# Picking the last pairs' expert results on TensorE instead of gathering them, with the shared experts split around the rounds

## The chip, the cores and the metric

The kernel runs on one core of a Trainium2 chip. The metric is the device time of one execution in microseconds (us); lower is better. Every time below comes from the hardware profiler or from timed runs on the chip.

## What is computed

One tower with three stages, all in float32. Stage one is a masked tokenizer, stage two a small attention layer, stage three a mixture of experts with top-2 routing and two shared experts:

```python
W = weight * mask[None]                       # (16, 5000, 128)
h = einsum('bg,egp->bep', x, W) + bias        # 64 batches x 16 tokens x 128
h = h + attention(layernorm(h))               # 8 heads, causal over 16 tokens
xf = layernorm(h).reshape(-1, 128)            # 1024 tokens
scores = sigmoid(xf @ gate_w.T)               # 64 experts, top 2 each
y[e] = (silu(buf[e] @ w1[e]) * (buf[e] @ w3[e])) @ w2[e]
routed = sum over the 2 experts of y * score * 2.5 / sum of the 2 scores
shared = (silu(xf @ sw1) * (xf @ sw3)) @ sw2
out = h + shared + routed
```

## The kernel before, in words

It is written in direct per-engine programs: each of the five engines (TensorE `pe`, VectorE `dve`, ScalarE `act`, GpSimd `pool`, SyncE `sp`) has its own list of instructions, which it runs strictly in the order in which they are written. The engines wait for each other by semaphores alone. A late instruction therefore holds all that stands behind it on its engine.

The 1024 tokens are eight **pairs** (chunks of 128 tokens, `NCH = 8`). In the tail of the program j, k and l are pairs 5, 6 and 7. The tokenizer streams 65 MB of weights through a ring buffer, masks them on VectorE and GpSimd and sums them on TensorE (L843) until about 157 us. The attention and the routing of earlier pairs run beside it. What is left then is the attention of pairs 6 and 7, the routing of pairs 5 to 7, and the experts.

**Routing.** For each pair VectorE picks the top two experts (`choose`), TensorE counts ranks (`rank_tokens`), VectorE computes for each token two slot numbers (`place`), and GpSimd scatters the token rows by indirect DMA to these slots in device memory (`scatter`, L486). SyncE loads the slots back (`load_slots`, L399).

**The experts run in two rounds** of groups of 512 slots. Round one (groups 0 to 7) has pairs 0 to 4 with 64 slots per expert, round two (groups 8 to 11) has pairs 5 to 7 with 32 slots per expert. Each group goes through: `turn_xs` (transpose on TensorE, L989 or in round two L993), `copy_xsT` (ScalarE, L696), `up` (L1015), `silu` (ScalarE, L704 and L705), `mid` (gate product: GpSimd L508 in round one, VectorE L1411 in round two), `turn_mid` (L1029), `copy_midT` (L711), `down` (L1045), `copy_y` (L715), `store_group` (SyncE to device memory, L405). Pair 7 is not scattered: VectorE marks its slots as one-hot rows (`mark_slots`, L1361 and L1362) and TensorE adds its tokens into round two's transposed inputs (`add_last`, L999).

**Collecting.** GpSimd gathers each token's two result rows from device memory by indirect DMA (`gather`, L533, two per pair, 16 in all), round one's pairs when round one's stores have landed, pairs 5 to 7 when round two's stores have landed. VectorE multiplies by the weights and adds (`combine`, L1429 and L1430, two instructions per pair), SyncE writes out two pairs at a time with two DMAs (L430). The weights come from `score_exp` (ScalarE, L725) and `weights` (VectorE, L1417 to L1422).

**The shared experts** (`shared_up` L1056, `silu_shared` L721, `shared_mid` L1400, `shared_down` L1064, `add_shared` L1405) run in two halves of four pairs, both after the last `down`. Their weights sw1, sw3 and sw2 arrive by three DMAs of SyncE (L415 to L417), which stand behind four `load_slots`, a piece of w2 (L389) and a 1 MB table of slot numbers (L414).

**The stretch around the change on TensorE** is `turn_xn(l)`, `turn_xs(0)`, `project(l)` (L865), `spin(3)`, `turn_xs(1)`, `spin(3)`, `turn_xs(2)`, `up(0)`, `up(1)`, `turn_xs(3)`, `turn_qk(l)`. `spin(n)` (L928) issues n matmuls whose result nobody reads. ScalarE has there `copy_xnT(l)` (L610), `copy_xsT(0)`, `copy_xsT(1)`, `square_qk(l)` (L599), `norm_qk(l)` (L605, L606), `probs(k)` (L641). `probs(k)` is the exponential that VectorE's `weigh_values(k)` (L1292, L1293) waits for. The norms' inverse square roots are powers on GpSimd (`root_*`, L455). In the trace a plain float32 matmul shows as two instructions (four calls of L993 are x8), a transpose as one (four calls of L989 are x4).

Of the kernel before, what the change touches and what calls it, by code (L numbers as in the profile page):

```python
# [19 lines left out]
ALU = mybir.AluOpType  # L20
# [7 lines left out]
P = 128  # L28
# [20 lines left out]
GATHERED_EARLY = NCH1  # L49
# [42 lines left out]
def M_BANK(g):  # L92
    return 4 if g < GROUPS1 else (3, 4)[g % 2]
# [6 lines left out]
def S_BANK(i):  # L100

    return ((1, 5, 7), (0, 2, 3))[i]
# [69 lines left out]
def tower_kernel(nc, x, tok_w, tok_b, tok_mask, W_dq, W_uq, W_qr, W_dkv, W_ukv, W_kr, W_o,  # L172
                 q_ln_g, q_ln_b, kv_ln_g, kv_ln_b, gate_w, w1, w3, w2, sw1, sw3, sw2, consts, masks, out):
    with ExitStack() as ctx:
# [8 lines left out]

        bank = [ctx.enter_context(nc.psum_tensor(f"bank{i}", [P, 512], F32)) for i in range(8)]
# [45 lines left out]
        wts = sb("wts", [P, NCH, 2])  # L230
        msel = sb("msel", [P, NCH, E], BF16)
# [21 lines left out]
        ssil, shs = ring_view(18304, 512), ring_view(18816, 512)  # L253

        hm = [mask[:, 256 * i:256 * (i + 1)].rearrange("p (i h) -> p i h", h=H) for i in range(2)]
        gt = [mask[:, 512 + 256 * i:768 + 256 * i].rearrange("p (i h) -> p i h", h=H) for i in range(2)]
        slot_iota, hot = xT[:, 0:M_SLOTS], prod[:, 0:M_SLOTS]
# [62 lines left out]
        s_iota, s_hot = sem("slot_iota_in"), sem("last_slots_marked")  # L320

# [31 lines left out]
        def _(sp):  # L353
# [59 lines left out]
            load_w2(0, (0, WREM), (0, S))  # L413
            sp.dma_start(slot_iota, masks[:, M_W:M_W + M_SLOTS]).then_inc(s_iota, 16)  # L414
            sp.dma_start(sw13[:, 0, :], sw1).then_inc(s_sw, 16)  # L415
            sp.dma_start(sw13[:, 1, :], sw3).then_inc(s_sw, 16)
            sp.dma_start(sw2s, sw2).then_inc(s_sw, 16)  # L417
            for g in range(STORED_FIRST):
                store_group(g)
# [3 lines left out]
            for g in range(STORED_FIRST, GROUPS):  # L423
                store_group(g)
# [20 lines left out]
        def _(pool):  # L445
            pool.memset(half[:], -0.5).then_inc(s_pool, 1)
            pool.memset(zeros, 0.0).then_inc(s_zsrc, 1)
            pool.wait_ge(s_ones, 1)
# [67 lines left out]
            root_h2(j)  # L516
            mid(0)
            mid(1)
            mid(2)
# [6 lines left out]
            scatter(k)  # L526
            root_h2(l)
            mid(7)

# [8 lines left out]
            pool.wait_ge(s_slot, NCH - 1)  # L538
            pool.wait_ge(s_yout[0], 16 * GROUPS1)
            for j in range(GATHERED_EARLY):  # L540
                gather(j)
            pool.wait_ge(s_ys, GROUPS)
            for j in range(GATHERED_EARLY, NCH1):
                gather(j)
            pool.wait_ge(s_gidx, 1)
            pool.wait_ge(s_yout[1], 16 * (GROUPS - GROUPS1))
            for j in range(NCH1, NCH):
                gather(j)

        @block.scalar  # L550
        def _(act):
# [155 lines left out]
            def copy_midT(g):  # L707
# [3 lines left out]
                act.copy(hT[g % 2], bank[M_BANK(g)][:, 0:PG * H]).then_inc(s_hT, 1)  # L711
# [106 lines left out]
        def _(pe):  # L818
# [201 lines left out]
            def turn_mid(g):  # L1020
                pe.wait_ge(s_hm, g + 1)
                if g >= 1:
                    pe.wait_ge(s_hT, g if g <= GROUPS1 else g - 1)
# [531 lines left out]
```

## Time and profile before

| what | us |
|---|---|
| median of 3 timed runs (lowest, highest) | 241.35 (240.23, 242.11) |
| the profiled execution, its own time | 241.4 |
| its span, first to last instruction | 239.7 |
| TensorE busy / VectorE busy / GpSimd busy | 184.3 / 152.4 / 145.6 |
| last tokenizer matmul | about 157 |
| last `down` matmul of round two | about 220.3 |

The span leaves out 1.7 us that the profiled execution has around it (241.4 - 239.7). Times in rows count from the span's start. Rows of a timeline or of the chain of waits read: start, duration, engine, line.

### The profile page before, as it was taken

The page shows a single profiled execution, that of the slowest core. Times are in us where ns is not written, and L with a number is a line of the kernel's source. Part 1 is how long each engine was busy: PE and PEld are TensorE (multiplying, and loading weights), DVE is VectorE, ACT ScalarE, POOL GpSimd, SP SyncE. Part 2 cuts the span into 40 slices and gives each one's busy share as a digit, 9 for nine tenths or more (in the row PEclk, how much of TensorE's full clock was granted, in tenths as well). Part 3 has the DMA queues.
Part 4 walks back from the last instruction along what each step waited for, and adds up shares of the span by engine and source line. Part 5 has one row for each costly group of instructions (what it writes and reads, how often), then busy time and mean ns, then how long its engine had stood idle before and what let it go on. Part 6 is the DMA issues. An engine that isn't in the chain of part 4 may idle for free.

```text
span 239.7 us, 6216 instructions
## 1 busy us (share of the span) xinstructions
PE 184.3 (77%) x2549; PEld 154.8 (65%) x2549; DVE 152.4 (64%) x366; ACT 82.7 (35%) x245; POOL 145.6 (61%) x117
## 2 busy tenths in 40 slices
PE   0057969558989969979879789699997989999700
PEld 0056949457878958857758767588776767767400
DVE  0024384686497796897996994978999627410571
ACT  2005200003324324324133124136878744344400
POOL 3326469519998949879969949620161651375360
PEclk9999997977999989999999999999999999999975
DMA  6989999999999999999999999949901329234241
GB/s 220 290 311 417 362 419 384 346 421 415 421 413 417 420 418 420 414 427 418 403 408 228 234 218 191 153 87 303 263 0 44 115 68 296 68 98 121 71 112 35
DMA packets 32982, 65.12 MB, mean 272 GB/s; under 512 B 2874, under 2 KB 25367, under 8 KB 32375
## 3 DMA queue, kind: packets, MB, share of 16 engines
q1 hardware_dynamic: 31416, 59.47, 75.0%
q10 hardware_dynamic: 576, 3.26, 3.4%
q0 software_dynamic: 960, 1.97, 3.1%
q8 instruction: 21, 0.34, 0.6%
q14 instruction: 9, 0.07, 0.1%
HBM read 56.96 MB, written 7.73 MB: 270 GB/s over the span
## 4 chain that ended last, share of the span: by engine, by line
PE 32%; DVE 24%; DMA 18%; SPq 9%; ACT 6%; issue 5%; POOL 3%; POOLq 1%; DVEq 0%; ACTq 0%
DMA ring<-in_L_tok_weight_dram 16%; PE bank L843 10%; DVE ring L1241 5%; SPq L362 4%; DVE bank L1271 4%; PE bank L1045 3%; DVE prod L1262 3%; PE bank L1015 3%; DVE prod L1293 2%; DVE bank L1301 2%; SPq L368 2%; PE bank L993 2%; PE bank L999 2%; PE bank L928 2%; POOL rstd L455 2%
## 5 line engine op out<-in xcount | busy, mean ns | idle before, releaser
L466 POOL TENSOR_TENSOR ring<-ring,mask 128x896 f32<-128x896 f32 (+1 forms) x48 | 91.5, 1935 | 18.7 <-DMA ring<-in_L_tok_weight_dram 18.6
L843 PE MATMUL bank<-ring,xT 128*64 128x128 f32 x1248 | 84.3, 294 | 11.3 <-DVE ring L1241 8.0
L843 PEld LDWEIGHTS bank<-ring,xT 128*64 128x64 f32 x1248 | 76.4, 149 | 16.0 <-DVE ring L1241 12.8
L1241 DVE TENSOR_TENSOR ring<-ring,bank 128x1024 f32<-128x1024 f32 (+1 forms) x45 | 45.8, 1049 | 35.4 <-DMA ring<-in_L_tok_weight_dram 35.4
L455 POOL TENSOR_TENSOR rstd<-mv,half 128x1 f32<-128x1 f32 (+1 forms) x24 | 14.4, 603 | 32.4 <-DVE mv L1249 21.5
L533 POOL DMA_INDIRECT ring<-expert_outputs,slot_index x16 | 16.2, 1010 | 16.6 <-DMA expert_outputs<-ring 12.4
L824 PE MATMUL bank<-cst,w 64*128 64x64 f32 x39 | 5.3, 328 | 15.6 <-DMA w<-in_x_dram 14.8
L486 POOL DMA_INDIRECT expert_inputs<-xf,slot_index x14 | 14.3, 1022 | 4.3 <-issue 3.5
L508 POOL TENSOR_TENSOR mask<-ring,mask 128x256 f32<-128x256 f32 x8 | 7.5, 938 | 14.4 <-ACT ring L705 11.4
L824 PEld LDWEIGHTS bank<-cst,w 64*128 64x128 f32 x39 | 5.0, 219 | 15.7 <-issue 14.8
L579 ACT ACTIVATE offset<-shift,rstd 128x1 f32<-128x1 f32 x16 | 4.7, 292 | 25.1 <-POOL rstd L455 25.1
L1015 PE MATMUL bank<-w,ring 128*64 128x128 f32 (+1 forms) x256 | 12.9, 277 | 0.5 <-ACT ring L705 0.4
L1045 PE MATMUL bank<-w2p,ring 64*64 64x128 f32 (+1 forms) x256 | 12.8, 272 | 0.3 <-ACT ring L715 0.2
L1271 DVE TENSOR_REDUCE bank<-prod 128x16 f32<-128x288 f32 (+7 forms) x8 | 12.1, 1511 | 0.3
L1015 PEld LDWEIGHTS bank<-w,ring 128*64 128x64 f32 (+1 forms) x256 | 10.1, 123 | 2.6 <-ACT ring L696 1.1
L1045 PEld LDWEIGHTS bank<-w2p,ring 64*64 64x64 f32 (+1 forms) x256 | 10.2, 120 | 2.3 <-issue 1.2
L1293 DVE TENSOR_TENSOR prod<-vcat,bank 128x256 f32<-128x256 f32 (+7 forms) x8 | 10.8, 1344 | 0.0
L1301 DVE TENSOR_REDUCE bank<-prod 128x128 f32<-128x256 f32 (+7 forms) x8 | 10.6, 1321 | 0.0
L1262 DVE TENSOR_TENSOR prod<-kcat,bank 128x256 f32<-128x256 f32 (+5 forms) x6 | 6.5, 1089 | 4.8 <-ACT vcat L635 4.8
L1336 DVE MAX8 top<-bank 128x8 f32<-128x64 f32 x8 | 1.9, 232 | 12.0 <-PE bank L914 12.0
L715 ACT COPY ring<-bank 128x512 f32<-128x512 f32 x12 | 7.0, 585 | 7.0 <-PE bank L1045 7.0
L928 PE MATMUL bank<-cst 128*128 128x128 f32 x70 | 9.4, 279 | 0.0
(153 smaller groups left out, 297.4 us busy)
## 6 DMA issues: line engine op xcount, KB each, us to landing
ring<-in_L_tok_weight_dram SPq DMA_DIRECT2D x48, 832.0 KB, 13.5
expert_inputs<-w ACTq DMA_DIRECT2D x3, 1024.0 KB, 10.6
ring<-expert_inputs SPq DMA_DIRECT2D x6, 512.0 KB, 5.4
expert_outputs<-ring SPq DMA_DIRECT2D x12, 256.0 KB, 2.7
mask<-in_L_tok_mask_dram SPq DMA_DIRECT2D x3, 832.0 KB, 15.6
w<-in_x_dram SPq DMA_DIRECT2D x1, 1250.0 KB, 13.0
w2p<-in_L_ffn_w_dram SPq DMA_DIRECT2D x1, 1024.0 KB, 19.2
xT<-masks_dram SPq DMA_DIRECT2D x1, 1024.0 KB, 8.1
```

Of the source, the lines that this page charges most:

```text
L455: pool.tensor_tensor(rstd[:, a:b], mv[:, a:b, 1], half[:, 0:b - a], ALU.pow).then_inc(s_rstd, 1)
L466: pool.tensor_tensor(unit(j, q, SPLIT(q // 2), UC), unit(j, q, SPLIT(q // 2), UC), mask[:, (m + SPLIT(q // 2)) * D:(m + UC) * D], ALU.mult ...
L486: pool.indirect_dma_start(out=xs_dram[j // NCH1], out_offset=bass.IndirectOffsetOnAxis(ap=s_idx[:, j, k:k + 1], axis=0), in_=xf[:, j, :], ...
L533: pool.indirect_dma_start(out=yg[:, 2 * j + k, :], out_offset=None, in_=ys_dram[r], in_offset=bass.IndirectOffsetOnAxis(ap=s_idx[:, j, k:k ...
L843: last = pe.matmul(bank[0][64 * par:64 * par + 64, 0:D], xT[:, (UC * t + c) * B:(UC * t + c + 1) * B], unit(j, 2 * t + par, c, c + 1), sta ...
L928: pe.matmul(bank[where][:, 256:256 + P], ident, ident, start=True, stop=True)
L1015: last = pe.matmul(bank[U_BANK(g)][row:row + slots, tile * P:(tile + 1) * P], xsT[g % 2][:, n * slots:(n + 1) * slots], w13[:, EXPERT(g, n ...
L1045: last = pe.matmul(bank[Y_BANK(g)][row:row + slots, tile * D:(tile + 1) * D], hT[g % 2][H * par:H * par + H, tile * H + col:tile * H + col ...
L1241: dve.tensor_tensor(both(j, t, a, b), both(j, t, a, b), m.rearrange("p (u f) -> p u f", u=1).to_broadcast([P, 2, (b - a) * D]), ALU.mult). ...
L1271: then(dve.tensor_reduce(raw(j).rearrange("p (h s) -> p s h", h=NH), prod[:, 0:n * f].rearrange("p (s h d) -> p s h d", h=NH, d=DK), AX.X, ...
L1293: then(dve.tensor_tensor(prod[:, 0:n * D].rearrange("p (h d s) -> p h d s", d=DH, s=n), vcat[:, :, 0:n].rearrange("p (h d) s -> p h d s", ...
L1301: then(dve.tensor_reduce(o_raw(j), prod[:, 0:n * D].rearrange("p (f s) -> p f s", f=D), AX.X, ALU.add))
```

## The change

Pairs 6 and 7 are no longer gathered. For each of them there is a table of 2048 slots by 128 tokens in device memory, zeroed by SyncE (1 MB each). ScalarE makes two diagonal matrices of the pair's weights (`weight_rows`), GpSimd scatters their rows to the token's two slots (`scatter_picks`), SyncE loads the table back (`load_picks`), and TensorE multiplies it with round two's results as they stand on chip (`pick`, 8 matmuls of 128x128 per group). The sum stays in a bank, and VectorE adds it to the residual in one instruction. GpSimd's gathers are pairs 0 to 4 and then pair 5. The exponential for the late weights becomes a power on GpSimd (`late_exp`), `weights` is run for pairs 5 and 6 and then for pair 7, both earlier than before. The first half of the shared experts moves into round one: `shared_up(0)` before `turn_xs(0)`, its product to GpSimd, `shared_down(0)` behind `rank_tokens(k)`. Round two's transposes use `is_transpose=True`. The DMAs of sw1 and sw3 move ahead of the w2 piece, sw2 ahead of the slot table.

```diff
 # SyncE
+            sp.dma_start(sw13[:, 0, :], sw1).then_inc(s_sw, 16)
+            sp.dma_start(sw13[:, 1, :], sw3).then_inc(s_sw, 16)
             load_w2(0, (0, WREM), (0, S))
+            sp.dma_start(sw2s, sw2).then_inc(s_sw, 16)
             sp.dma_start(slot_iota, masks[:, M_W:M_W + M_SLOTS]).then_inc(s_iota, 16)
-            sp.dma_start(sw13[:, 0, :], sw1).then_inc(s_sw, 16)
-            sp.dma_start(sw13[:, 1, :], sw3).then_inc(s_sw, 16)
-            sp.dma_start(sw2s, sw2).then_inc(s_sw, 16)
+            sp.wait_ge(s_nopick, 1)
+            for table in pick_dram:
+                sp.dma_start(table..., no_picks...).then_inc(s_pickz, 16)
...
+            for g in range(STORED_FIRST, GROUPS1):
+                store_group(g)
+            load_picks(0)
+            sp.wait_ge(s_prod, NCH)
+            load_picks(1)
+            for g in range(GROUPS1, GROUPS):
                 store_group(g)
 # GpSimd
+            pool.memset(no_picks, 0.0).then_inc(s_nopick, 1)
             mid(0)
             mid(1)
+            pool.wait_ge(s_ssil, 1)
+            pool.wait_ge(s_shg, 1)
+            pool.tensor_tensor(shs, ssil, shg, ALU.mult).then_inc(s_shs, 1)
...
             scatter(k)
+            late_exp(NCH1, NCH - 1)
             root_h2(l)
             mid(7)
+            late_exp(NCH - 1, NCH)
+            for j in LATE:
+                scatter_picks(j)
...
-            for j in range(NCH1, NCH):
-                gather(j)
+            gather(NCH1)
 # ScalarE
             copy_xnT(l)
+            square_qk(l)
             copy_xsT(0)
             copy_xsT(1)
-            square_qk(l)
             norm_qk(l)
...
             copy_midT(8)
+            weight_rows(NCH - 1)
             copy_xsT(9)
 # TensorE
                 if i == 0:
                     pe.wait_ge(s_sw, 48)
-                    pe.wait_ge(s_hm, GROUPS)
+                    pe.wait_ge(s_xfTs, 4)
...
             turn_xn(l)
-            turn_xs(0)
+            spin(2, 7)
             project(l)
-            spin(3, 7)
+            shared_up(0)
+            turn_xs(0)
+            spin(3, 1)
             turn_xs(1)
...
             rank_tokens(k)
+            shared_down(0)
             turn_mid(4)
...
-            shared_up(0)
             shared_up(1)
-            shared_down(0)
+            pick(8)
+            pick(9)
+            pick(10)
             shared_down(1)
+            pick(11)
 # VectorE
             mark_slots(8)
+            dve.tensor_copy(s_idx[:, l, :], last_slot[:]).then_inc(s_gidx, 1)
+            weights(NCH - 1, NCH)
             mark_slots(9)
...
-            for j in range(4, NCH):
-                combine(j)
+            combine(4)
+            combine(5)
+            dve.wait_ge(s_picked, 1)
+            dve.tensor_tensor(fin[:, LATE[0]:, :], hres[:, LATE[0]:, :],
+                              bank[PICKED]..., ALU.add).then_inc(s_fin, len(LATE))
```

On TensorE, at the start of round one, these rows stand between the transpose of pair 7's normed tokens (L861, L927 after) and the transpose of group 1's slots. Before:

```order
L861 MATMUL bank3<-cst,qkn 128x128 [waits qkv_copied,xn]
L989 MATMUL bank2<-cst,ring 128x128 [waits xs_in0]
L989 MATMUL bank2<-cst,ring 128x128 x3
L865 MATMUL bank3<-wproj,xnT 128x149 [waits xnT_copied]
L928 MATMUL bank7<-cst 128x128 x3
L989 MATMUL bank2<-cst,ring 128x128 [waits xsT_copied]
```

And after (L1130 is `shared_up`, L1055 `turn_xs`, L994 `spin`):

```order
L927 MATMUL bank3<-cst,qkn 128x128 [waits qkv_copied,xn]
L994 MATMUL bank7<-cst 128x128 x2
L931 MATMUL bank3<-wproj,xnT 128x149 [waits xnT_copied]
L1130 MATMUL bank4<-xfT,ring 128x512 [waits xfT_copied,shared_w_in]
L1130 MATMUL bank7<-xfT,ring 128x512
L1055 MATMUL bank2<-cst,ring 128x128 [waits xs_in0]
```

The first shared matmul, with its wait for the shared weights, now stands ahead of every transpose of round one.

On SyncE the same DMAs stand in another order after the four slot loads. After the change:

```order
L415 DMA ring<-expert_inputs_1 128x8x128 x3
L429 DMA ring<-in_L0_ffn_sw1_dram 128x128 [waits third_summed]
L430 DMA ring<-in_L0_ffn_sw3_dram 128x128
L405 DMA w2p<-in_L0_ffn_w2_dram 16x16x128
L432 DMA ring<-in_L0_ffn_sw2_dram 128x128
L433 DMA xT<-masks_dram 128x2048
```

The three shared weights are behind the slot loads as before, sw2 also behind the w2 piece, and all three ahead of the 1 MB table.

On VectorE, in the routing of pair 7, the pieces behind the first pair of one-hot marks are after the change:

```order
L1454 TENSOR_SCALAR prod<-xT,last_slot 128x512 [waits slots,slot_iota_in]
L1455 SCALAR_TENSOR_TENSOR prod<-xT,last_slot,prod 128x512 [waits vector_chain]
L1563 CAST slot_index<-last_slot 128x2
L1512 TENSOR_SCALAR ew<-ew 128x2 [waits late_top2_exp]
L1513 RECIPROCAL ew<-ew 128x2 [waits vector_chain]
L1514 SCALAR_TENSOR_TENSOR ew<-ew 128x1 [waits vector_chain]
L1515 RECIPROCAL ew<-ew 128x1 [waits vector_chain]
L1516 SCALAR_TENSOR_TENSOR wts<-ew 128x1 [waits vector_chain]
L1517 SCALAR_TENSOR_TENSOR wts<-ew 128x1 [waits vector_chain]
L1454 TENSOR_SCALAR prod<-xT,last_slot 128x512
```

Six small instructions of `weights` now stand between the marks of groups 8 and 9, and so ahead of `mid(8)`, which is still behind the last mark.

## Rows read from the trace of the kernel before

**Rows 1.** The page: busy time, share of the span and instructions of each engine

```profile
PE 184.3 (77%) x2549; PEld 154.8 (65%) x2549; DVE 152.4 (64%) x366; ACT 82.7 (35%) x245; POOL 145.6 (61%) x117
```

**Rows 2.** Chain of waits where the attention's tail meets round one

```profile
165.28 0.67 PE bank L928 x6
165.95 0.45 PE bank L989 x4
...
168.87 0.28 ACT bank L641
```

**Rows 3.** Slot loads (ns min/median/max, first and last start), then SyncE's timeline

```profile
L399 SPq DMA_DIRECT2D ring<-expert_inputs x4: 377/742/1726, 159.6 to 162.0; - x4
...
163.81 1.82 SPq L389 DMA_DIRECT2D w2p<-in_L_ffn_w_dram  x1
...
166.16 0.43 SPq L415 DMA_DIRECT2D ring<-in_L_ffn_sw_dram  x1
```

**Rows 4.** DMA issues 163.5 to 167 us: KB each, us from issue to landing

```profile
ring<-expert_inputs SPq DMA_DIRECT2D x1, 512.0 KB, 8.5
w2p<-in_L_ffn_w_dram SPq DMA_DIRECT2D x1, 128.0 KB, 7.5
...
ring<-in_L_ffn_sw_dram SPq DMA_DIRECT2D x2, 64.0 KB, 7.2
```

**Rows 5.** Windows: length, busy (count) PE PEld DVE ACT POOL, PEclk, DMA, GB/s

```profile
50.00:53.00 3.00, 2.63 (x26) 2.63 (x28) 2.64 (x7) 0.00 (x0) 0.21 (x1) 0.50 1.00 415
161.50:168.50 7.00, 6.75 (x66) 5.78 (x64) 5.78 (x9) 4.21 (x16) 0.70 (x1) 1.00 1.14 291
```

**Rows 6.** Timeline of TensorE: 36 like matmuls, twice, idle time before them in brackets

```profile
32.09 2.19 PE L843 MATMUL bank<-ring,xT 128*64 128x128 f32 x36 [0.30 <-DVE ring L1241]
50.37 3.65 PE L843 MATMUL bank<-ring,xT 128*64 128x128 f32 x36 [4.05 <-DVE ring L1241]
```

**Rows 7.** Groups by form after 150 us: busy us, mean ns, idle before

```profile
L1056 PE MATMUL bank<-xfT,ring 128*128 128x512 f32 x8 | 3.7, 605 | 0.0
L1064 PE MATMUL bank<-ring 128*128 128x128 f32 x16 | 2.2, 281 | 1.4 <-DVE ring L1400 1.4
L582 ACT ACTIVATE xf<-hres,offset,rstd 128x128 f32<-128x128 f32 x3 | 1.5, 494 | 0.1
```

**Rows 8.** Timeline of GpSimd, 167 to 196 us

```profile
167.71 0.70 POOL L455 TENSOR_TENSOR rstd<-mv,half 128x2 f32<-128x2 f32 x1 [8.91 <-ACT square_junk L599]
...
193.00 1.01 POOL L486 DMA_INDIRECT expert_inputs<-xf,slot_index  x1 [0.79 <-DVE slot_index L1353]
...
195.30 0.59 POOL L455 TENSOR_TENSOR rstd<-mv,half 128x1 f32<-128x1 f32 x1
```

**Rows 9.** Chain of waits in round two, 200 to 208 us

```profile
200.78 1.09 PE bank L993 x8
...
206.96 0.61 PE bank L1029 x16
```

**Rows 10.** Timeline of all engines, 206 to 231 us

```profile
206.35 0.42 DVE L1411 TENSOR_TENSOR mask<-ring,bank 128x256 f32<-128x256 f32 x1
...
207.62 0.37 ACT L711 COPY ring<-bank 128x256 f32<-128x256 f32 x1 [1.30 <-PE bank L1029]
...
225.09 1.00 POOL L533 DMA_INDIRECT ring<-expert_outputs,slot_index  x1 [5.10 <-DMA expert_outputs<-ring]
...
229.28 0.16 DVE L1417 TENSOR_SCALAR ew<-ew 128x6 f32<-128x6 f32 x1
...
230.12 0.23 DVE L1422 SCALAR_TENSOR_TENSOR wts<-ew 128x3 f32<-128x3 f32 x2
```

**Rows 11.** Chain of waits at the end: store, last gather, last combine

```profile
221.00 3.25 DMA expert_outputs<-ring
...
231.61 2.91 DMA ring<-expert_outputs,slot_index
...
234.93 0.35 DVE ring L1430
```

More of the change, by code:

```diff
@@ L48 @@
 CAP = 256
-GATHERED_EARLY = NCH1
+LATE = range(NCH1 + 1, NCH)
 WREM = 16
@@ L526, in _, with late_exp, scatter_picks @@
             scatter(k)
+            def late_exp(first, last):
+                n = slice(first, last)
+                pool.wait_ge(s_inv, 1)
+                pool.wait_ge(s_top, last)
+                pool.tensor_tensor(ew[:, 0, n, :], inv_e[:, 0:last - first, :], top[:, n, 0:2], ALU.pow).then_inc(s_late_exp, 1)
+            def scatter_picks(j):
+                pool.wait_ge(s_diag, j - LATE[0] + 1)
+                pool.wait_ge(s_pickz, 16 * len(LATE))
+                pool.wait_ge(s_slot, j + 1)
+                if j == NCH - 1:
+                    pool.wait_ge(s_gidx, 1)
+                for k in range(2):
+                    pool.indirect_dma_start(
+                        out=pick_dram[j - LATE[0]], out_offset=bass.IndirectOffsetOnAxis(ap=s_idx[:, j, k:k + 1], axis=0),
+                        in_=diag[:, j - LATE[0], k, :], in_offset=None, bounds_check=ROWS[1] - 1,
+                        oob_is_err=False).then_inc(s_pscat[j - LATE[0]], 16)
+            late_exp(NCH1, NCH - 1)
             root_h2(l)
             mid(7)
+            late_exp(NCH - 1, NCH)
+            for j in LATE:
+                scatter_picks(j)
             def gather(j):
@@ L1065, in shared_down, with pick @@
                 last.then_inc(s_sh2, 1)
+            def pick(g):
+                pe.wait_ge(s_ys, g + 1)
+                for n in range(len(LATE)):
+                    if g == GROUPS1:
+                        pe.wait_ge(s_pick[n], 16)
+                    for i in range(PG):
+                        last = pe.matmul(bank[PICKED][:, n * D:(n + 1) * D], picks[n][:, PG * (g - GROUPS1) + i, :],
+                                         ys[:, PG * g + i, :], start=(g == GROUPS1 and n == 0 and i == 0),
+                                         stop=(g == GROUPS - 1 and n == len(LATE) - 1 and i == PG - 1))
+                if g == GROUPS - 1:
+                    last.then_inc(s_picked, 1)
             j, k, l = NCH - 3, NCH - 2, NCH - 1
@@ L1415, in weights @@
                 n = slice(first, last)
-                dve.wait_ge(s_exp, 1 if first == 0 else 2)
+                if first == 0:
+                    dve.wait_ge(s_exp, 1)
+                else:
+                    dve.wait_ge(s_late_exp, 1 if last < NCH else 2)
                 then(dve.tensor_scalar(ew[:, 1, n], ew[:, 0, n], 1.0, None, ALU.add))
```

94 lines of the change are left out of this document (62 added, 32 removed).

## The prediction, on record before the run

> **What bounds the kernel now.** I read the page first. TensorE is busy for 77% of the span and VectorE for 64% [rows 1]; no engine is full, so order and waits decide, and I follow the chain of waits from 160 us on. It has three parts. Until about 188 us it is the attention of the last two pairs. TensorE transposes group 1's slots at 165.95 us, ScalarE copies them and only then norms pair 7 and takes pair 6's exponential at 168.87 us [rows 2]; VectorE starts on pair 6's values with that. From 200 us on TensorE itself is the chain (round two). From 221.00 us it is the tail: the last store lands 3.25 us later, six gathers follow each other on GpSimd, the last starts at 231.61 and lands after 2.91 us, and the last combine ends at 235.28 us [rows 11]. Two output DMAs then take 4.4 us up to the span's end at 239.7.
>
> **What the change takes out.** Before, GpSimd waited 5.10 us for round two's stores and then issued six gathers. From the first at 225.09 to the sixth at 231.61 us are five steps, so 1.30 us each [rows 10, 11]. After, only two stand there; four scatters of pick rows stand earlier. This is the gain that the change is built for: four steps, at most 5.2 us.
>
> **The wait that it adds, round one.** `shared_up(0)` now stands on TensorE ahead of every transpose of round one, and it waits for all three shared weights. When are they there? SyncE issues four slot loads, the last at 162.0 us, the w2 piece at 163.81 us, and, before the change, sw1 at 166.16 us [rows 3]. The last slot load takes 8.5 us (lands 170.5), the w2 piece 7.5 us (lands 171.3), the shared weights 7.2 us (sw1 lands about 173.5) [rows 4]. Every DMA in this stretch is late because the queue is full: 2 MB of slots at 291 GB/s in 512-byte rows [rows 5]. Moving sw1 and sw3 up by 2.4 us of issue does not pass them by the slots, and sw2 is still behind the w2 piece. 128 KB of sw1 and sw3 and 64 KB of sw2 at 291 GB/s are 0.7 us, so sw2 lands at 171.3 + 0.7 = 172.0 us. Low end 170.5 (where the last slots land), high end 173.5 (where sw1 lands today).
>
> The Trainium skill ("DMA: Bandwidth & Descriptors", Queues, rings and completion order) says that each of the 16 engines takes its descriptors in ring order, but that completion is not first in, first out per issuing engine. By this the weights could overtake the w2 piece, though not the slots; the trace agrees in that sw1, issued behind the 1 MB table, lands 0.3 us before it. That would make the wait end near the low end, and the result 1.5 us better.
>
> TensorE ends `project(l)` at 165.28 us [rows 2] and then stands still for 6.7 us. Everything behind is held: the transposes, so `copy_xsT(1)` on ScalarE, so `norm_qk(l)` and `probs(k)` queued behind it, so VectorE. Then, in order: `shared_up(0)` 1.85 us (half of 3.7 [rows 7]), four transposes 0.45, three spins 0.67, and `turn_xs(1)` can start.
>
> The clock adds to it. After 4.05 us of idle time 36 matmuls took 3.65 us, at full clock 2.19, so 1.46 us more [rows 6]; the granted clock there was 0.50, 1.2 GHz [rows 5]. With the half clock lasting to the end of a stretch like that I take 1.6 us; bounds 0 and 1.9.
>
> Sum: 172.0 + 1.85 + 1.6 + 0.45 + 0.67 = 176.57 against 165.95: **+10.6 us** for TensorE. VectorE's path is shorter (`square_qk(l)` now stands ahead of the two copies) and comes +9 late, but its next step, pair 7's keys, waits for `turn_qk(l)` and `qkv(l)`, which stand behind `turn_xs(3)`: so +10 there too. TensorE has small waits for other engines behind this point, and some of the delay is made up there. No single row prices that; I take 1.0 back (bounds 0 and 2): **+9.6**, bounds with those of landing and clock +7.5 and +12.
>
> **Before pair 7's norm.** GpSimd scatters pair 6 at 193.00 us, and pair 7's root comes at 195.30 behind the second scatter, 1.2 us after its input was ready [rows 8]. `late_exp` for four columns now stands in between. A power over one column is 0.59 us, over two 0.70 [rows 8]; 0.15 a column more is about 1.0 (bounds 0.6 and 1.3). `shared_down(0)`, 1.1 us [rows 7], stands ahead of `turn_mid(4)` and `turn_o(l)`; GpSimd's `mid(6)` waits for the former, so the scatter comes some 0.4 us later. Together **+1.4**. GpSimd's product for the shared half and its memset stand where it waits for ScalarE anyway, as in the 8.91 us before 167.71 [rows 8]: nothing. Unhidden, the product would cost at most some 2 us.
>
> **Round two.** As transposes the four `turn_xs` are x4 instead of x8: 0.45 against 1.09 us [rows 2, 9], at most 2.6 us gained. But two of them are followed by something else that is late: `add_last(8)` waits for VectorE's marks, and `turn_mid(8)` at 206.96 [rows 9] for `mid(8)`, which started at 206.35 [rows 10]. In front of `mid(8)` VectorE now has six weight instructions, 1.07 us from 229.28 to 230.35 in today's place [rows 10], with an extra wait about 1.2. So `turn_mid(8)` comes 1.2 us later, the third short transpose gives 0.65 back, and the last `down` ends **+0.55** late (bounds -2.0 and +1.2). It doesn't decide the end, GpSimd does.
>
> **The tail.** GpSimd's second pick scatter waits for ScalarE's diagonals, behind `copy_midT(8)` (207.62 [rows 10], + 1.2 = 208.8). That copy takes 0.4, two scaled copies of 128x128 at 0.49 each [rows 7]: 210.2. Then come 14 indirect DMAs in a row, the last starts 13 x 1.30 = 16.9 us later, at 227.1 + 0.1. It isn't held by the stores: the last lands at 220.85 + 0.7 + 3.2 = 224.8. The gather lands 2.91 later at 230.1, `combine(5)` takes 0.73, so 230.8. Output is 4.4 us as before and 1.0 for two more DMAs behind the same combine, so 236.2 against 239.7: **-3.5** (bounds -5.2 and -2). TensorE's side of the tail is shorter: 220.85 + 1.85 + 32 pick matmuls, four groups at 1.09, + 1.1 is 228.2. The pick table of pair 7 is issued at about 214 and is 1 MB of 512-byte rows, 3.6 us at 291 GB/s, so in by 219.5, before `pick(8)` at 222.7. The zeroing (2 MB written) follows the loads on the queue, in a stretch where nobody waits for a DMA: nothing.
>
> **Sum.** 239.7 + 9.6 + 1.4 - 3.5 = 247.2 us of span; with the 1.7 us around it 248.9. The profiled execution (241.4) is the median of the runs (241.35), so this stands for the median too. What a measurement of this kernel can tell from no change is about 1% (2.4 us).
>
> **Rivals.**
> 1. The shared weights are there in time (by 165.3 us). Only `shared_up(0)` with the rest lies in the way: 165.28 + 2.97 = 168.25, +2.3, no clock loss. 239.7 + 2.3 + 1.4 - 3.5 + 1.7 = 241.6: the same. For it: the change puts them further ahead. Against it: the 8.5 us of the slot load that stands before them [rows 4].
> 2. Not slower, by the tail: weights in time, VectorE's path alone decides in round one (`probs(k)` comes +0.9 late since the norm no longer waits for squares), `late_exp` is 0.6 and hidden by half, and the tail gives the full 5.2. 239.7 + 0.9 + 0.5 - 5.2 + 1.7 = 237.6. It decides if the wait on the shared weights ends before about 166 us; each microsecond later costs one, so the break-even with before is at about 169 us of landing, without the clock.
> 3. The pick tables come late on top: if pair 7's load landed 12 us after its issue, at 226 instead of 219.5, picks and `shared_down(1)` would end at 226 + 4.4 + 1.1 = 231.5, 0.7 us after `combine(5)`. With a held queue of stores 2 us in all: 250.9.
>
> **How the numbers follow.** The forecast's case has 0.72, of which a little (landing and clock at their low ends, more made up than I take) reaches down to 243.5. Rival 1 has 0.12, rival 2 has 0.11, rival 3 0.05. The forecast's own range, by the bounds of its terms, is 244.5 to 251. To leave out no more than 2 in 10 the range reaches down to rival 1: 241.0 to 251.0. Faster by over 1%: rival 2 and a little of rival 1, 0.13. Within 1%: 0.14. Slower by over 1%: 0.73.
>
> **What would show it.** In the trace after: TensorE idle for 5 to 8 us right before the two shared matmuls, released by the DMA of the shared weights; a granted clock of 0.5 behind it; VectorE idle for some 8 us before pair 6's values; pair 7's keys at about 184 us (174.5 before). Then a GpSimd row without gaps from about 220 to 237 us, and pick matmuls that wait for nothing. The prediction is wrong if the shared matmuls start by 167 us, or if the time between the last tokenizer matmul and `turn_o(l)` doesn't grow.

## The result, and the profile after the change

| kernel | median us (lowest to highest) | span of the profiled execution |
|---|---|---|
| before | 241.73 (240.23 to 243.15) | 239.7 |
| after | 254.24 (253.03 to 255.41) | 253.7 |

The changed kernel takes 1.052 times as long, 95% interval 1.044 to 1.060. The forecast was 248.9 us, in a range of 241.0 to 251.0: the sign and the main mechanism came true, the size did not. The profiled execution of the changed kernel took 255.41 us, 1.2 more than the median.

The page of the changed kernel, busy time and the granted clock in 40 slices of 6.3 us:

```profile
PE 193.9 (76%) x2601; PEld 161.4 (64%) x2601; DVE 153.8 (61%) x368; ACT 82.6 (33%) x248; POOL 149.7 (59%) x122
...
PEclk9999979959999889999999999986967999999997
```

TensorE is busy 9.6 us longer than in [rows 1], with 52 instructions more. The digits 6, 9, 6 and 7 in the 28th to 31st slice (from 171 us) are two stretches of half clock, not one. The chain of waits there:

```profile
163.59 1.82 SPq L429
166.40 5.20 DMA ring<-in_L_ffn_sw_dram
171.65 3.78 PE bank L1130 x4
```

This is the wait that was forecast: the third shared weight, issued at 166.40, lands 5.20 us later, and `shared_up(0)` (L1130) starts at 171.65 (forecast 172.0). The loads of sw1 and sw3, the w2 piece and sw2 land in their order of issue here; no overtaking shows. What TensorE does from there on (start, duration, line; idle time before it in brackets):

```profile
171.65 3.78 PE L1130 MATMUL bank<-xfT,ring 128*128 128x512 f32 x4 [6.49 <-DMA ring<-in_L_ffn_sw_dram]
175.22 0.96 PE L1055 MATMUL bank<-cst,ring 128*128 128x128 f32 x4
...
176.85 0.66 PE L1055 MATMUL bank<-cst,ring 128*128 128x128 f32 x4
...
185.47 0.66 PE L960 MATMUL bank<-wukv,ckvT 85*64 85x128 f32 x8 [0.69 <-ACT kcat L683]
186.61 1.98 PE L1082 MATMUL bank<-w,ring 128*64 128x128 f32 x16 [0.49 <-ACT ring L758]
...
190.29 1.97 PE L1082 MATMUL bank<-w,ring 128*64 128x128 f32 x16
192.19 1.03 PE L1055 MATMUL bank<-cst,ring 128*128 128x128 f32 x4
```

The same two transposes, `turn_xs(1)` and `turn_xs(5)`, in the kernel before:

```profile
165.79 0.60 PE L989 MATMUL bank<-cst,ring 128*128 128x128 f32 x4
...
178.17 0.66 PE L989 MATMUL bank<-cst,ring 128*128 128x128 f32 x4
```

The four wide matmuls take 3.78 us at half clock, and `turn_xs(1)` starts at 176.85: +11.06 us (forecast +10.6). Then comes what was not forecast. Shortly before `up(2)` at 186.61 us the clock falls again, for some 7 us: 16 matmuls take 1.98 us there, and 1.09 where the clock is full. `turn_xs(5)` at 192.19 is 14.0 us late. The windows show both falls (window, its length, busy time of TensorE with its count, granted clock, DMA share, GB/s):

```profile
165.00:170.00 5.00, 0.15 (x2) 0.91 1.28 268
170.00:175.00 5.00, 3.35 (x4) 0.50 0.94 373
175.00:178.00 3.00, 2.99 (x21) 0.84 0.94 384
...
187.00:190.00 3.00, 3.00 (x32) 0.50 0.00 0
190.00:193.00 3.00, 3.00 (x28) 0.50 0.00 0
```

Between them, from 178 to 184 us, it is back at 1.00.

Other engines waited as expected. Two lines of the waits after 160 us (what waits and its line, what released it: us in all, times, longest):

```profile
DVE mx L1385 <- ACT bank L694: 12.5, 2, 10.0
...
PE bank L1130 <- DMA ring<-in_L_ffn_sw_dram: 6.5, 1, 6.5
```

Behind it GpSimd and round two. `late_exp` (L567) stands between the second scatter of pair 6 and pair 7's root, where [rows 8] had nothing:

```profile
208.57 0.97 POOL L517 DMA_INDIRECT expert_inputs<-xf,slot_index  x1 [0.30 <-issue]
209.56 1.06 POOL L567 TENSOR_TENSOR ew<-inverse_e,top 128x4 f32<-128x4 f32 x1
210.59 0.54 POOL L486 TENSOR_TENSOR rstd<-mv,half 128x1 f32<-128x1 f32 x1
```

The end of TensorE's work:

```profile
223.09 0.68 PE L1099 MATMUL bank<-cst,mask 64*64 64x64 f32 x16 [1.55 <-DVE mask L1503]
...
234.68 0.68 PE L1099 MATMUL bank<-cst,mask 64*64 64x64 f32 x16 [1.07 <-ACT ring L765]
...
237.82 1.98 PE L1130 MATMUL bank<-xfT,ring 128*128 128x512 f32 x4
239.64 1.05 PE L1149 MATMUL bank<-ring,mask 128*128 128x128 f32 x8
...
246.78 1.06 PE L1149 MATMUL bank<-ring,kcat 128*128 128x128 f32 x8
```

`turn_mid(8)` waits 1.55 us for VectorE's `mid(8)` (in [rows 9] the same instruction, L1029, starts at 206.96; this one is 16.1 us late). `turn_mid(11)` waits 1.07 us for ScalarE, and the two last `down` behind it take 2.5 us up to `shared_up(1)`, 1.9 in the kernel before. The last `down` ends at 237.8, 17.5 us late. And the picks (L1149) are eight blocks of eight matmuls, 0.89 us from one to the next, not four at 1.09 as I had counted: 7.1 us. `shared_down(1)` (L1139, at 245.00) stands behind six of these blocks. The last gathers are not what the end waits for:

```profile
239.88 0.99 POOL L592 DMA_INDIRECT ring<-expert_outputs,slot_index  x1 [0.30 <-issue]
242.44 0.99 POOL L592 DMA_INDIRECT ring<-expert_outputs,slot_index  x1 [1.56 <-DMA expert_outputs<-ring]
243.74 0.99 POOL L592 DMA_INDIRECT ring<-expert_outputs,slot_index  x1 [0.30 <-issue]
```

GpSimd is not in one unbroken row up to here, as was forecast; it waits 1.56 us for the stores, which [rows 10] shows as 5.10. After the last gather's issue at 243.74 TensorE picks until 247.8. VectorE first waits 2.29 us for `shared_down(1)`, comes to pair 5's gathered rows at 247.54 without waiting, and to the picked rows at 248.19:

```profile
246.09 0.69 DVE L1497 TENSOR_TENSOR hres<-hres,bank 128x512 f32<-128x512 f32 x1 [2.29 <-PE bank L1139]
...
248.19 0.41 DVE L1579 TENSOR_TENSOR ring<-hres,bank 128x256 f32<-128x256 f32 x1
```

### The profile page after: what moved, and what is told of

Read it like the earlier page. It is cut to its first block, busy times and chain, and to the rows that moved or that the text cites. A ratio compares the mean times of both kernels' runs of the same rounds, so it can differ in the third digit from the quotient of the medians.

```text
span 253.7 us, 6344 instructions
## 1 busy us (share of the span) xinstructions
PE 193.9 (76%) x2601; PEld 161.4 (64%) x2601; DVE 153.8 (61%) x368; ACT 82.6 (33%) x248; POOL 149.7 (59%) x122
## 4 chain that ended last, share of the span: by engine, by line
PE 33%; DVE 20%; DMA 13%; SPq 11%; POOL 8%; ACT 7%; issue 6%; DVEq 0%; ACTq 0%; POOLq 0%
DMA ring<-in_L_tok_weight_dram 9%; PE bank L909 8%; PE bank L1082 5%; DVE ring L1334 5%; SPq L378 4%; POOL ring L497 4%; PE bank L1116 3%; DMA expert_inputs<-xf,slot_index 2%; PE bank L1130 2%; PE bank L1149 2%; DMA ring<-in_L_ffn_sw_dram 2%; PE bank L1099 2%; DVE bank L1364 2%; POOL rstd L486 2%; SPq L384 2%
## 5 line engine op out<-in xcount | busy, mean ns | idle before, releaser
L909 PE MATMUL bank<-ring,xT 128*64 128x128 f32 x1248 | 82.0, 289 | 11.5 <-DVE ring L1334 7.7
L909 PEld LDWEIGHTS bank<-ring,xT 128*64 128x64 f32 x1248 | 74.0, 146 | 16.4 <-DVE ring L1334 12.5
L539 POOL TENSOR_TENSOR mask<-ring,mask 128x256 f32<-128x256 f32 x8 | 6.9, 865 | 29.5 <-ACT ring L758 23.5
L890 PE MATMUL bank<-cst,w 64*128 64x64 f32 x39 | 5.3, 328 | 16.6 <-DMA w<-in_x_dram 15.9
L1082 PE MATMUL bank<-w,ring 128*64 128x128 f32 (+1 forms) x256 | 14.6, 295 | 1.4 <-ACT ring L758 1.0
L890 PEld LDWEIGHTS bank<-cst,w 64*128 64x128 f32 x39 | 5.0, 219 | 16.7 <-issue 15.9
L592 POOL DMA_INDIRECT ring<-expert_outputs,slot_index x12 | 12.0, 1002 | 4.9 <-issue 3.3
L1082 PEld LDWEIGHTS bank<-w,ring 128*64 128x64 f32 (+1 forms) x256 | 11.6, 134 | 3.6 <-issue 1.6
L1099 PE MATMUL bank<-cst,mask 64*64 64x64 f32 x192 | 8.6, 231 | 3.7 <-ACT ring L765 2.0
L1099 PEld LDWEIGHTS bank<-cst,mask 64*64 64x64 f32 x192 | 7.1, 141 | 5.8 <-issue 2.9
L1130 PE MATMUL bank<-xfT,ring 128*128 128x512 f32 x8 | 5.8, 860 | 6.5 <-DMA ring<-in_L_ffn_sw_dram 6.5
L1394 DVE TENSOR_REDUCE bank<-prod 128x128 f32<-128x256 f32 (+7 forms) x8 | 10.6, 1322 | 0.0
## 6 DMA issues: line engine op xcount, KB each, us to landing
w<-in_x_dram SPq DMA_DIRECT2D x1, 1250.0 KB, 14.1
w2p<-in_L_ffn_w_dram SPq DMA_DIRECT2D x1, 1024.0 KB, 17.5
```

The source lines that it names most:

```text
L592: pool.indirect_dma_start(out=yg[:, 2 * j + k, :], out_offset=None, in_=ys_dram[r], in_offset=bass.IndirectOffsetOnAxis(ap=s_idx[:, j, k:k ...
L909: last = pe.matmul(bank[0][64 * par:64 * par + 64, 0:D], xT[:, (UC * t + c) * B:(UC * t + c + 1) * B], unit(j, 2 * t + par, c, c + 1), sta ...
L1082: last = pe.matmul(bank[U_BANK(g)][row:row + slots, tile * P:(tile + 1) * P], xsT[g % 2][:, n * slots:(n + 1) * slots], w13[:, EXPERT(g, n ...
L1099: last = pe.matmul(bank[b][rows, at + i * H:at + (i + 1) * H], hm[g % 2][rows, i, :], ident[rows, rows], start=True, stop=True)
L1130: last = pe.matmul(bank[S_BANK(i)[a]][:], sw13[:, a, :], xfT[:, 512 * i:512 * i + 512], start=True, stop=True)
```

## The experiments

Theory: the loss is one wait, TensorE's for weights that stand in the queue behind 2 MB of slots, and what follows from it; the rest of the change is small. Rivals: the picks and the work added around pair 7's norm cost as much; or the clock is the larger part. Ratios are to the kernel before on the same chip, with their 95% interval; the kernel before took 240.5 to 241.5 us there.

**The early half moved behind the landing.**

```
             project(l)
-            shared_up(0)
             turn_xs(0)
...
             turn_o(k)
+            shared_up(0)
             values(l)
```

> The change with shared_up(0) moved behind turn_o(k), where the shared weights have landed; all else as after. If the wait for the shared weights and the half clock that follows it make the 12.5 us, TensorE's clock stays full from 165 us on, turn_xs(1) starts near 168 instead of 176.85, and the time falls by 14.1 less 1.2 for the shared matmuls in front of values(l): 241 to 242 us. If the late part (late_exp, the marks, the pick scatters) or contention from the 4 MB of pick tables makes it, the time stays above 249 us.

242.47 us, ratio 1.007 (1.003 to 1.011). The granted clock is 1.00 in every window from 160 to 196 us, and the chain of waits shows `turn_xs(1)` at 165.54, the four shared matmuls in 1.73 us, and `up(2)` at full speed:

```profile
165.54 0.66 PE bank L1055 x4
...
173.45 1.73 PE bank L1130 x4
...
176.50 1.09 PE bank L1082 x16
```

One line moved takes back 4.4 of the 5.2 per cent, 10.7 us. What is left, 1.8 us, belongs to the rest of the change and to the early half in its new place.

**The idle time filled.** 28 more multiplications of the identity ahead of `shared_up(0)`: `+            spin(28, 1)`.

> The change with 28 more spins (6.2 us at full clock) between project(l) and shared_up(0): TensorE waits as long, but not idle. The first shared matmul still starts at about 171.7. If the half clock costs what the rows say, the first four shared matmuls take 1.98 instead of 3.78 us and the time falls by 1.8 us (252.4). If the second stretch of half clock (186 to 193 us) is a consequence of the first, it falls by 4.9 us (249.3). If the clock has no part in it, 254.2.

251.51 us, ratio 1.046 (1.040 to 1.053). The wait is the same, the clock isn't:

```profile
164.11 6.41 PE L994 MATMUL bank<-cst 128*128 128x128 f32 x56
170.75 1.98 PE L1130 MATMUL bank<-xfT,ring 128*128 128x512 f32 x4 [0.22 <-DMA ring<-in_L_ffn_sw_dram]
...
183.59 1.09 PE L1082 MATMUL bank<-w,ring 128*64 128x128 f32 x16 [0.49 <-ACT ring L758]
```

The identities are the first row. The shared matmuls take 1.98 instead of 3.78 us: 1.8 in this profile. By the two ratios the clock is worth 1.3 us, with overlapping intervals. So by the times most of the loss is the wait itself. The second fall is absent from this profile too, and its span is 6.3 us shorter than the changed kernel's (247.4 against 253.7). But it is the fastest of five executions (249.14 us) and the one with the highest mean granted clock (0.971, the others 0.954 to 0.966), and the median shows no 5 us gained. Whether the clock falls in the other four is not known.

**The wait alone, in the kernel before.** The loads in the changed order and the wait ahead of `turn_xs(0)`, nothing else:

```
             project(l)
+            pe.wait_ge(s_sw, 48)
             turn_xs(0)
```

> The kernel before with two edits only: the shared weights' DMAs in the order of the change, and a wait for them on TensorE between project(l) and turn_xs(0); no shared matmul moves. By the wait alone turn_xs(1) starts 8 us late (6.4 of wait, 1.8 of half clock), so 249 to 250 us, and 252 if the clock falls a second time. If the shared matmuls or ScalarE's extra work behind them are what costs, it stays under 244 us.

251.01 us, ratio 1.041 (1.033 to 1.048): +9.9 us with no shared matmul, pick or norm changed.

```profile
172.05 1.11 PE L989 MATMUL bank<-cst,ring 128*128 128x128 f32 x4 [6.32 <-DMA ring<-in_L_ffn_sw_dram]
...
184.31 1.92 PE L1015 MATMUL bank<-w,ring 128*64 128x128 f32 x16
```

The second fall (16 matmuls in 1.92 us) is here as well, from 182.9 to 189.8 us. The profiled execution (252.64 us) is the slowest of four.

**Both shared halves at the end, the picks kept.** `shared_up(0)` and `shared_down(0)` stand behind `down(11)`; ScalarE's and GpSimd's parts of the early half go back with them.

> The change without the split of the shared experts: both halves run after the last down as before, with the picks, the late powers, the round two transposes and the order of round two as after. Late steps cost 1.0 (late_exp) + 0.9 (marks) + 1.1 (turn_mid(10) first) - 0.6, TensorE's end is 3.7 + 5.4 + 1.1 us behind the last down: 239 to 241 us. If the picks themselves are a loss, above 244 us.

243.97 us, ratio 1.013 (1.007 to 1.019): 3 us above the expected range. The expectation had 10.2 us (3.7 + 5.4 + 1.1) from the last `down` to the end of TensorE's work; in the profile it is 12.6, since the picks take 7.1. The clock also falls here, from 176.7 to 180.1 us, without a stall. The difference to the first experiment, 0.6% (1.4 us), would be what the early half is worth when well placed, but the intervals overlap: it isn't shown.

**TensorE's old order for `turn_mid(10)`.** In the kernel of the first experiment:

```
-            turn_mid(10)
             down(9)
+            turn_mid(10)
             turn_mid(11)
```

> The kernel with shared_up(0) moved behind turn_o(k) (242.47 us), and in it turn_mid(10) stands behind down(9) again, as before the change. Theory: the 1.07 us that turn_mid(11) waits for ScalarE's copy_midT(10), which stands behind copy_y(9), is on the path and comes from that exchange alone: down(9) fills the gap, and the time is 241.4 us, with no wait at turn_mid(11) in the trace. Rival: something behind it (the picks, the last stores) takes the time up, and it stays at 242.4 us.

243.08 us, ratio 1.008 (1.005 to 1.011), against 1.007: nothing gained in the median.

```profile
222.51 0.68 PE L1099 MATMUL bank<-cst,mask 64*64 64x64 f32 x16 [0.56 <-ACT ring L765]
223.12 2.35 PE L1116 MATMUL bank<-w2p,ring 64*32 64x128 f32 x64
```

The wait only shrinks, to 0.56 us; the two last `down` behind it take 2.35 us, where they take 1.95 in the kernel of the next experiment. The theory missed in that TensorE's order is not what makes the wait. That ScalarE's order of copies makes it is tried in the last experiment.

**What stands before pair 7's norm and before `mid(8)`.** In the kernel of the first experiment:

```
-            late_exp(NCH1, NCH - 1)
             root_h2(l)
+            late_exp(NCH1, NCH - 1)
...
-            weights(NCH - 1, NCH)
             mark_slots(9)
             mark_slots(10)
             mark_slots(11)
             mid(8)
+            weights(NCH - 1, NCH)
```

> The kernel with shared_up(0) moved behind turn_o(k) (242.47 us), and in it late_exp of pairs 5 and 6 stands behind root_h2(l) on GpSimd, and weights(7) behind mid(8) on VectorE. Theory: the first takes 1.0 us of GpSimd's power from the path to pair 7's norm, the second six small VectorE operations (about 1.1 us) from the path to turn_mid(8), which waits 1.55 us now: 240.5 us, with that wait near 0.5 us. Rival: pair 7's norm is on the path but turn_mid(8) would wait as long for the marks: 241.5 us. Other rival: neither decides, 242.4 us.

240.32 us, ratio 0.996 (0.992 to 1.000): 1.1% less than without the edits, 2.6 us, a little more than the two prices together.

```profile
208.91 0.68 PE L1099 MATMUL bank<-cst,mask 64*64 64x64 f32 x16 [0.54 <-DVE mask L1503]
```

The wait at `turn_mid(8)` falls from 1.55 to 0.54 us.

**Both edits.**

> Both edits of the two kernels before it together. If the three prices add up (1.1 + 1.0 + 1.1 of 242.47 us), 239.3 us, 0.5% under the kernel before the change, and pair 7's results picked by TensorE are then worth having. If they overlap, 240.5 us, which can't be told from the kernel before.

240.09 us, ratio 0.995 (0.992 to 0.998), as the norm edits alone within the intervals; the three prices (3.2 us in all) don't add up, since the order's is missing.

**The same kernel with gathers in place of the picks.** The tables, their zeros, scatters, loads, the pick matmuls and their last addition are left out; `gather(6)` and `gather(7)`, `combine(6)` and `combine(7)` are back.

> The kernel with both edits, without the picks: pairs 5, 6 and 7 are gathered by GpSimd as before the change, and the weight tables, their zeros, scatters and loads are left out; the first shared half stays early. Theory: six gathers behind the last store set the end. In the kernel with the move alone the last store landed at 230.8 us; less 3.2 us for the edits, five more issues of 1.30 us, one of 1.0 and a landing of some 2.9 us give an end of the gathers at 238 us where the picks end at 232.5, so 4 to 5 us more than the kernel with the picks: 243.5 us. Rival: the picks only move work from GpSimd to TensorE at the same price: within 1 us of the kernel with them.

243.06 us, ratio 1.007 (1.004 to 1.010): the picks are worth 1.2%, 3.0 us; the theory was right in kind and 1 to 2 us too high. GpSimd's last two gathers and VectorE's last combine here:

```profile
226.83 1.00 POOL L582 DMA_INDIRECT ring<-expert_outputs,slot_index  x1 [4.61 <-DMA expert_outputs<-ring]
...
233.34 1.00 POOL L582 DMA_INDIRECT ring<-expert_outputs,slot_index  x1 [0.30 <-issue]
```

The last gather starts 6.5 us behind the first. With the picks two gathers follow the stores (the last starts at 229.94 in the kernel of both edits), and TensorE's picks end at 233.4.

**The gaps before the second fall filled.** In the changed kernel:

```
             turn_o(k)
+            pe.wait_ge(s_sil, 1)
+            spin(5, 1)
             values(l)
+            spin(4, 1)
             up(2)
```

> The changed kernel, in which TensorE multiplies the identity nine times more, five before values(l) and four before up(2): the engine idles there for 0.69 and 0.49 us after the stall, and then the granted clock falls a second time, for some 6 us. Theory: that second fall follows from these gaps so soon after the stall, and costs 3 us: filled, the clock stays at 1.00 from 177 us on and the time is 251 us. Rival: the second fall comes after the stall whatever TensorE does there: 254 us, and the clock falls to 0.50 near 187 us as before.

254.22 us, ratio 1.055 (1.048 to 1.062). The profile goes by the theory, the time by the rival:

```profile
184.00:187.00 3.00, 2.91 (x35) 1.00 0.00 0
187.00:190.00 3.00, 3.00 (x40) 1.00 0.00 0
```

The clock stays at 1.00, but the nine spins are longer than the gaps: `up(2)` starts 16.0 us after `shared_up(0)`, 15.0 before. In the profiled execution the end came 80.4 us after `shared_up(0)`'s start, 82.1 in the changed kernel; the medians don't show this gain. As it is one profile, it doesn't show that the gaps are the cause of the fall either.

**The weights loaded first.** In the changed kernel SyncE issues them ahead of the wait for the scatters:

```
-            sp.wait_ge(s_tok, 3 * (NCH - 1))
+            sp.wait_ge(s_tok, 3 * NCH)
+            sp.dma_start(sw13[:, 0, :], sw1).then_inc(s_sw, 16)
+            sp.dma_start(sw13[:, 1, :], sw3).then_inc(s_sw, 16)
+            sp.dma_start(sw2s, sw2).then_inc(s_sw, 16)
             sp.wait_ge(s_scat[0], 16 * 2 * NCH1)
             for i in range(GROUPS1 // 2):
                 load_slots(0, i)
```

> The changed kernel, in which SyncE issues the three loads of the shared weights before it waits for the first round's scatters, ahead of the four slot loads, not behind them; TensorE's order is the changed kernel's. Theory: the loss is the place in the queue alone: the weights land before 165 us, TensorE waits for nothing, no fall of the clock follows, the slots come at most 0.5 us later, and the time is that of the kernel with shared_up(0) moved behind turn_o(k), 242.5 us. Rival: the slot loads come later by what the weights take (2 us or more), turn_xs(0) waits for them in the shared half's place and the clock falls all the same: 246 us or more.

244.66 us, ratio 1.011 (1.006 to 1.015). The queue is shown to be the cause from the other side. The DMA issues from 158 to 168 us (KB each, us to landing), and TensorE's timeline, where nothing is waited for:

```profile
ring<-in_L_ffn_sw_dram SPq DMA_DIRECT2D x3, 64.0 KB, 2.4
```

```profile
166.22 1.88 PE L1129 MATMUL bank<-xfT,ring 128*128 128x512 f32 x4
```

The same 64 KB take 2.4 us ahead of the slots and 5.2 behind them. The time is 2 us above the theory's 242.5 and below the rival's 246. The ten executions lie in two groups: four took 242.1 to 242.8 us at mean granted clocks of 0.975 to 0.984, six 244.3 to 246.2 at 0.952 to 0.970, and the profiled one of these (246.19) has the clock at 0.50 from 214.2 to 217.6 us. A fall of the clock in the tail may be what is left; that isn't shown.

**The small edits around `turn_xs` alone, in the kernel before.** The turns of round two as transposes, `project(l)` ahead of `turn_xs(0)`, the spins at their new places.

> The kernel before, with only the changed kernel's small edits around turn_xs: the turns as TensorE transposes, project(l) ahead of turn_xs(0), and the spins at their new places. Theory: 36 instructions of the same kind and length as before, full clock: the time of the kernel before within 0.5%. Rival: the chip does not take transposes for work, and the clock falls more often in the stage of the first round: over 1% slower than before, which would also be behind the 244 us of the kernel with the picks alone.

241.74 us, ratio 1.000 (0.996 to 1.004): together they change nothing in the time. In the profile the short transposes do give something, 0.5 us between `turn_mid(8)` and the last `down` (12.9 against 13.4). But it also shows the clock at 0.50, from 173.7 to 180.4 us, without a stall before it, and `turn_xs(5)` 2.3 us later than in the kernel before. Such falls may hide a gain in the median; that isn't shown. One window of it:

```profile
175.00:178.00 3.00, 3.00 (x30) 0.50 0.00 0
```

**Early loads with the norm edits.**

> The kernel with the weights' loads ahead of the slot loads, and late_exp of pairs 5 and 6 behind root_h2(l), weights(7) behind mid(8). If the early loads are worth what the move was worth, it takes what the kernel with both edits took, 0.5% less than the kernel before; if the early loads cost the slots something, as much more; a gain over 1% on the kernel before is not expected.

241.27 us, ratio 0.999 (0.996 to 1.002), against 0.996 (0.992 to 1.000) for the moved line with the same edits: the two ways can't be told apart.

**The changed kernel and the kernel before again.**

> The changed kernel again, as it is, for a second profile. If the second fall of the granted clock belongs to the stall, it shows again between 185 and 193 us, up(2) takes 1.9 us, and turn_xs(5) starts some 14 us later than in the kernel before. If it was of that execution alone, up(2) takes 1.1 us and turn_xs(5) comes 11 us later; the median stays near 1.052 of the kernel before either way.

253.76 us, ratio 1.051 (1.046 to 1.057), and the second fall is there again:

```profile
173.59 3.38 PE L1130 MATMUL bank<-xfT,ring 128*128 128x512 f32 x4 [7.54 <-DMA ring<-in_L_ffn_sw_dram]
...
187.84 1.97 PE L1082 MATMUL bank<-w,ring 128*64 128x128 f32 x16
```

> The kernel before again, as it is, for a second profile. If its clock falls now and then in the same stretch (174 to 193 us) without any stall, as in the kernel with the small edits around turn_xs alone, the falls belong to this stage of any of these kernels and are not the change's doing. The ratio is 1.00 within 0.5%, which also shows how well the ratios of this study can be told apart.

241.47 us, ratio 1.000 (0.997 to 1.003); full clock from 160 to 200 us, as in the first profile.

**ScalarE's two copies exchanged.** In the kernel with the norm edits:

```
-            copy_y(9)
             copy_midT(10)
+            copy_y(9)
             copy_midT(11)
```

> The kernel with shared_up(0) moved, late_exp and weights(7) moved (240.3 us), and in it ScalarE's copy_midT(10) stands ahead of copy_y(9). Theory: turn_mid(11)'s wait comes from ScalarE's order; with the copies exchanged it goes, TensorE has its eighth of work behind it 1.07 us earlier, and since TensorE alone sets the end the time is 239.3 us, 0.9 to 1.0% less than the kernel before. Rival: the time behind it is taken back (down(11) waits for copy_y(9), now late), 240.3 us.

239.99 us, ratio 0.994 (0.991 to 0.997). `turn_mid(11)` no longer waits:

```profile
218.49 0.68 PE L1099 MATMUL bank<-cst,mask 64*64 64x64 f32 x16
219.11 1.95 PE L1116 MATMUL bank<-w2p,ring 64*32 64x128 f32 x64
```

From `turn_mid(8)` to `shared_up(1)` TensorE now needs 12.9 us, 14.1 with the norm edits alone, so the wait was ScalarE's order. The time lies between theory (239.3) and rival (240.3): the ratios give 0.2% (0.5 us), with overlapping intervals. VectorE shows where a part goes: its last combine waits for a gather, so both sides of the tail end together.

```profile
231.03 0.35 DVE L1526 SCALAR_TENSOR_TENSOR ring<-ring,wts,hres 128x128 f32<-128x128 f32 x1 [0.24 <-DMA ring<-expert_outputs,slot_index]
```

It is the best version of the study: 0.6% under the kernel before, small, but no change lies outside its interval.

## Why the prediction was right and wrong

**Right: the wait and its price.** The landing (171.65 us against 172.0), the 6.5 us of idle TensorE, the half clock behind it, VectorE's 10.0 us of waiting for pair 6's exponential, `turn_xs(1)` at +11.06 against +10.6. The Trainium skill's rule that I had set beside it ("DMA: Bandwidth & Descriptors", Queues, rings and completion order), that a later load may finish first, would have ended the wait near 170.5. That didn't happen: the four loads landed in their order of issue. The rule itself stands, since in the kernel before sw1 did land 0.3 us ahead of the 1 MB table issued before it, as the prediction read. The experiments settle the cause from three sides: the wait alone in the kernel before costs 9.9 us, the moved matmuls give back 10.7, early loads give back 4.1% (9.9 us).

**Wrong: "some of the delay is made up there ... I take 1.0 back".** Nothing was made up. In both profiles of the changed kernel and in that of the wait alone the clock fell again near `up(2)`, and `turn_xs(5)` came 14.0 us late instead of 9.6. That term is 4.4 us too small in the profiled execution: 0.46 was there at `turn_xs(1)`, 1.0 was not regained, 2.96 were lost on top, 2.5 of them between `up(2)` and `turn_xs(5)` at half clock. How much of it stands in the median is open: the two kernels whose profiles show a stall but no second fall were 1.3 us faster (the spins ahead) and no faster (the gaps filled, which itself cost 1 us). Of the nine executions of the changed kernel the five with a mean granted clock of 0.940 to 0.942 took 253.8 to 256.6 us, the four with 0.948 to 0.961 took 253.0 to 254.0: this hints that the second fall is not in all of them, but falls elsewhere in the program move the mean too. What makes the clock fall a second time is open too.

**Wrong: "It doesn't decide the end, GpSimd does".** I sized TensorE's side of the tail with 32 pick matmuls in "four groups at 1.09". That is the price of a row of eight in [rows 9], but the 32 calls are 64 instructions in the trace, 16 in each group, and they take 7.1 us in place of 4.4. That alone lifts TensorE's side from 228.2 to 230.9, level with GpSimd's 230.8. The last `down`, for which I had +0.55 behind the first two delays, came later as well: `turn_mid(11)` waits 1.07 us for ScalarE's `copy_midT(10)`, a wait that I had not looked for since TensorE's own order seemed to help, and the two last `down` took 0.6 us more than before. The third short transpose gave 0.5 of its 0.65 us. So TensorE set the end: six blocks of picks, `shared_down(1)` behind them, and VectorE's additions. The last gather was there when VectorE came to it, though "It isn't held by the stores" failed too: GpSimd waited 1.56 us for them.

**Right by luck: the tail's -3.5.** From the last `down` to the end it is 15.9 us now (253.7 - 237.8) and was 19.4 (239.7 - 220.3): -3.5. But it was argued from GpSimd's queue, and against its own last `down` (220.85) the forecast end (236.2) was 15.4 us, so -4.0. Against gathers, and all else equal, the picks gave 3.0 us.

**Right: pair 7's norm.** `late_exp` took 1.06 us against 1.0, and VectorE's weights delayed `mid(8)`; moved away, both gave 2.6 us where their terms (1.0 and 1.2) had 2.2.

**The sum.** Span 247.2 forecast, 253.7 measured. How late TensorE is, point by point:

| point | forecast | measured | miss |
|---|---|---|---|
| `turn_xs(5)` | +9.6 | +14.0 | 4.4 |
| `turn_mid(8)` (+1.4 and +1.2 in the forecast) | +12.2 | +16.1 | 3.9 |
| end of the last `down` | +11.55 | +17.5 | 6.0 |
| end of the span | +7.5 | +14.0 | 6.5 |

So 4.4 us are the wait, the clock and what was not made up; pair 7's terms then came 0.5 us less than forecast; 2.1 are ScalarE's wait, the longer `down` and the smaller gain of the transpose; and 0.5 is the tail, where the longer picks count only as far as they exceed GpSimd's side. In medians the miss is 5.3 us. The range ended at 251.0 since every term's bound behind the wait was small or negative; a loss there, like a second fall of the clock, had no bound.

**The rivals.** None of the three came true. The condition of the first two, weights in time, was made in two experiments: Rival 1 had 0.1% over the kernel before (241.6 against 241.35), the moved line takes 0.7% and the early loads 1.1%. Rival 3's picks never waited for their tables. Rival 2 asked for the tail's full 5.2 us; with the waits taken away too, 240.0 is the best that was measured, not 237.6.

## What to carry to other kernels

Before a matmul that needs a load is moved ahead of others, read the landing of that load, behind all that its queue holds, not its issue: here one line placed 8 us too early cost 10.7 us. When work moves from one engine to another, count its instructions in the program and size both sides of the tail again, since the bound changes hands. When a chain is late, look for what the wait brings with it (the clock, a copy in another engine's order) before assuming that slack absorbs it.

## What the runs showed of the hardware

- After a stall of 6.3 to 7.5 us the granted clock was 0.50 until about 176 us, and in three profiles (the changed kernel twice, the wait alone) it fell to 0.50 a second time, 10, 10 and 7 us later, for 7 us. It did not in the one profile with the stall filled by spins, nor in the one with the two small gaps ahead of `up(2)` filled. It also fell near that place without any stall in two others (the small edits alone, the picks alone), so the stall is not its only cause. The Trainium skill ("TensorE: Matmul & The Clock Gate", A second HAM failure mode: psum-queue depth-cycling) tells of short idle times between groups of matmuls that make the clock go to and fro. The gaps of 0.69 and 0.49 us fit it in part. That the kernel with filled stall has the same two gaps and no fall does not fit, nor that the clock fell ahead of the 0.49 us gap in the repeat of the changed kernel, and in the wait alone after gaps of only 0.44 and 0.19 us.
- 64 KB took 2.4 us from issue to landing ahead of 2 MB of slot loads and 5.2 behind them.
- Four turns took 0.59 us from their start to the next instruction as transposes, and 1.09 as plain matmuls, both at full clock. With the other small edits they changed nothing in the time of the kernel before.
